# Attention tiles in blocks of 128 neighbouring edges, the feed-forward gathers issued first, and h turned a step later, in a graph network in f32 on one core

## The reference, cut to what matters

```python
# layer 0: attention over edges, softmax over the edges of each dst, then feed-forward
q, k, v = x @ qW + qb, x @ kW + kb, x @ vW + vb
scores = sum(q[src] * k[dst], heads) / 4 + edge_attr @ eW + eb
attn = softmax of scores over the edges with the same dst
out = segment_sum(v[src] * attn, dst) @ oW + ob
x = layer_norm(x + out, ln1_g, ln1_b)
h = gelu(layer_norm(x @ f1W + f1b, lnf_g, lnf_b)) @ f2W + f2b
x = layer_norm(x + h, ln2_g, ln2_b)
# layer 2: h = x @ lin_w.T + lin_b, then three times
agg = segment_sum((h @ weight[i])[src], dst)
h = gru_cell(agg, h)         # r, z = sigmoid(...), n = tanh(in + r * hn), h = (1 - z) * n + z * h
```

## Time and profile before

| what | value |
|---|---|
| median of 3 runs | 6031.04 us (6014.32 to 6034.06) |
| the profiled execution, its own time | 6028.9 us |
| its span, first to last instruction | 6027.0 us |
| attend, about | 210 to 800 us |
| ffn, about | 815 to 1925 us |
| gate0, gate1, gate2, about | 3340 to 3975, 3975 to 4590, 4590 to 5320 us |
| busy in the whole span | PE 71%, DVE 68%, POOL 60%, ACT 49% |
| mean granted clock of PE | 0.867 of full speed |

### The profile page before, as it was taken

One profiled execution on the slowest core, in us unless ns is written; L12 is line 12 of the kernel. 1 busy time (PEld: TensorE's weight loads), 2 busy tenths in 40 slices (PEclk: granted clock), 3 DMA queues, 4 the chain that ended last, 5 costly groups with the idle time before them and its releaser, 6 DMA issues. The chain is left out here.

```text
span 6027.0 us, 75672 instructions
## 1 busy us (share of the span) xinstructions
PE 4279.1 (71%) x16190; PEld 2524.1 (42%) x16190; DVE 4070.7 (68%) x13522; ACT 2924.8 (49%) x6388; POOL 3629.7 (60%) x3234
## 2 busy tenths in 40 slices
PE   6577759999997556546665679967996669836643
PEld 3244434444443333334443445534443334336643
DVE  6576659999997444457775676557665889836633
ACT  0466637777775010146665345534443446536643
POOL 4676558888885888735555660056104757855355
PEclk8788869999998777778887899988998899977877
DMA  6233323333332444456665675457545667757621
GB/s 214 66 85 80 73 70 99 99 99 99 99 99 78 62 62 63 54 141 196 193 190 162 185 211 146 131 160 214 164 141 147 176 159 211 197 162 227 183 78 54
DMA packets 767598, 802.43 MB, mean 133 GB/s; under 512 B 139632, under 2 KB 527800, under 8 KB 767018
## 3 DMA queue, kind: packets, MB, share of 16 engines
q1 hardware_dynamic: 405354, 393.44, 23.5%
q0 software_dynamic: 117504, 209.42, 15.0%
q10 hardware_dynamic: 244288, 194.72, 9.7%
HBM read 445.32 MB, written 351.92 MB: 132 GB/s over the span
## 5 line engine op out<-in xcount | busy, mean ns | idle before, releaser
L462 PE MATMUL gate_bank<-gate_ht,gate_whh 128*128 128x512 f32 x1764 | 874.6, 618 | 32.5 <-DVE gate_n L532 22.2
L925 POOL DMA_INDIRECT xh<-mean_xh,mean_pos_all x392 | 378.0, 964 | 349.0 <-DVE mean_xh L1027 158.9
L462 PEld LDWEIGHTS gate_bank<-gate_ht,gate_whh 128*128 128x128 f32 x1764 | 341.3, 202 | 413.0 <-issue 381.6
L2053 PE MATMUL back_ps_sums<-back_same,back_rows 128*128 128x512 f32 x400 | 289.5, 890 | 285.7 <-DMA back_rows<-x_a,back_idx 285.7
L151 POOL DMA_INDIRECT ffn_rows<-att_sums,ffn_idx x392 | 409.0, 1043 | 114.8 <-issue 106.3
L289 POOL DMA_INDIRECT gate_rows<-h_a,by_pos x200 | 195.8, 979 | 433.3 <-POOLq L117 327.3
L1494 PE MATMUL ffn_ps_f<-ffn_hg,ffn_f 128*128 128x512 f32 x784 | 407.1, 616 | 46.4 <-ACT ffn_hg L1671 46.4
L458 PE MATMUL gate_bank<-by_rank,gate_win 128*128 128x512 f32 x882 | 435.1, 593 | 0.0
L1487 PE MATMUL ffn_ps_u<-ffn_xs_t,ffn_up_w 128*128 128x512 f32 x784 | 387.2, 596 | 1.1 <-issue 1.1
L583 ACT ACTIVATE gate_z<-gate_bank,gate_b_rz 128x512 f32<-128x512 f32 x294 | 201.5, 686 | 351.0 <-PE gate_bank L462 221.0
L2034 POOL DMA_INDIRECT back<-back_out,back_dest x200 | 324.3, 1621 | 68.0 <-issue 60.1
(11 more groups left out here) (270 smaller groups left out, 11984.1 us busy)
## 6 DMA issues: line engine op xcount, KB each, us to landing
mean_x<-x_a SPq DMA_DIRECT2D x196, 256.0 KB
back<-blank ACTq DMA_DIRECT2D x99, 264.0 KB, 4.6
mean_rows<-back SPq DMA_DIRECT2D x98, 264.0 KB
hp<-mean_xh SPq DMA_DIRECT2D x98, 264.0 KB
gate_x<-xh SPq DMA_DIRECT2D x98, 264.0 KB
gate_hot<-hot_rows SPq DMA_DIRECT2D x100, 256.0 KB
ffn_x<-in_x_in SPq DMA_DIRECT2D x98, 256.0 KB
ffn_xr<-in_x_in SPq DMA_DIRECT2D x98, 256.0 KB
```

The source lines that it names most:

```text
L462: last = nc.tensor.matmul(bank_[:, :], whh[:, c * D:(c + 1) * D], ht[:, t.slot4, :], start=not inputs, stop=True)
L925: nc.gpsimd.indirect_dma_start(out=g["xh"][:, :], out_offset=bass.IndirectOffsetOnAxis(ap=pos_all[:, t.n, j:j + 1], axis=0), in_=xh[:, t.n ...
L2053: last = nc.tensor.matmul(ps_sums[t.slot][:, :], rows[:, t.slot4, j, :], same[:, t.slot, j, :], start=j == 0, stop=j == J - 1)
```

## The change

In attend, SP loads the indices from a new input `edge_blocks`, which holds the same edges so that gather j fetches the 128 neighbouring edges 128j to 128j+127. Transposes and out product then use dense columns, and the store of `att_sums` uses `part_tile`, four pieces of 512 bytes for each partition. In ffn, POOL's four gathers stand at the head of its step, and DVE makes `xh` with scalar_tensor_tensor, the inverse as a broadcast tensor operand, in the place of tensor_scalar. In the gates, the transposes of h, `out` and the stores move from lag 2 to lag 3, `hn` has four buffers, and in the final round what comes behind (power, shifts, scatter) moves a step too.

```diff
@@ gated_layer
-        d, hn = (f.sb(s, [P, 2, SUPER]) for s in ("d", "hn"))
+        d, hn = f.sb("d", [P, 2, SUPER]), f.sb("hn", [P, 4, SUPER])
...
-                if final and (t := item_at(5)):
+                if final and (t := item_at(6)):
                     ln.rstd(nc, pool, t, y_done)
                 if e := edges_at(0):
                     sums.gather(pool, e)
-                if final and (t := item_at(6)) and t.has:
+                if final and (t := item_at(7)) and t.has:
...
-                if t := item_at(2):
+                if t := item_at(3):
                     wait(pe, h_done, t.n + 1)
                     wait(pe, out_done, t.n)
                     for j in range(J):
                         last = nc.tensor.transpose(ps_out[:, j * D:(j + 1) * D],
-                                                   hn[:, t.slot, j * P:(j + 1) * P], g["ident"][:, :])
+                                                   hn[:, t.slot4, j * P:(j + 1) * P], g["ident"][:, :])
...
-                    wait(dve, h_turned, t.n - 1)
+                    wait(dve, h_turned, t.n - 3)
...
-                if not final and (t := item_at(2)):
+                if not final and (t := item_at(3)):
                     wait(act, h_turned, t.n + 1)
@@ attention_pass
-                                 nm_tile(g["by_dst"], t)).then_inc(idx_loaded[t.slot4], 16)
+                                 g["edge_blocks"][t.n]).then_inc(idx_loaded[t.slot4], 16)
...
-                        nc.tensor.transpose(edge_columns(ps_send[:, :])[:, j, :], send[:, t.slot4, j, :], g["ident"][:, :])
+                        nc.tensor.transpose(ps_send[:, j * P:(j + 1) * P], send[:, t.slot4, j, :], g["ident"][:, :])
...
-                        last = nc.tensor.matmul(ps_out[:, j * D:(j + 1) * D], edge_columns(att[:, t.slot, :])[:, j, :],
+                        last = nc.tensor.matmul(ps_out[:, j * D:(j + 1) * D], att[:, t.slot, j * P:(j + 1) * P],
                                                 ow[:, :], start=True, stop=True)
...
-                    act.dma_start(nm_tile(g["att_sums"], t), out[:, t.slot, :]).then_inc(stored[t.slot], 16)
+                    act.dma_start(part_tile(g["att_sums"], t.n, 0, D),
+                                  out[:, t.slot, :].rearrange("p (j d) -> p j d", j=J)).then_inc(stored[t.slot], 16)
@@ ffn_pass
             def step(tile_at):
+                if t := tile_at(0):
+                    gather_step(nc, pool, t, idx, rows, g["att_sums"], idx_loaded, a_done, gathered)
                 if t := tile_at(2):
...
-                if t := tile_at(0):
-                    gather_step(nc, pool, t, idx, rows, g["att_sums"], idx_loaded, a_done, gathered)
...
-                        last = nc.vector.tensor_scalar(xh[:, t.slot4, j, :], a[:, t.slot4, j, :],
-                                                       mv[:, root_slot(t, LN1), LN1, j, 0:1], inverse(t, LN1)[:, j:j + 1],
-                                                       ALU.subtract, ALU.mult)
+                        last = nc.vector.scalar_tensor_tensor(
+                            xh[:, t.slot4, j, :], a[:, t.slot4, j, :], mv[:, root_slot(t, LN1), LN1, j, 0:1],
+                            inverse(t, LN1)[:, j:j + 1].broadcast_to([P, D]), ALU.subtract, ALU.mult)
```

More of the change, by code:

```diff
@@ L372, in gated_layer @@
         ht_loaded = f.sems("ht_loaded", 4)
[L373 removed]
+        stored, ht_stored = f.sems("stored"), f.sems("ht_stored", 4)
         r_made, z_made, nh_made, ni_made, h_turned = (
@@ L415, in step @@
                     sums.store_hots(sp, e)
-                if final and (t := item_at(5)) and t.has:
+                if final and (t := item_at(6)) and t.has:
                     wait(sp, stored[t.m % 2], 16 * (t.m // 2 + 1))
@@ L420, in step @@
                                  ).then_inc(back_loaded[t.m % 4], 16)
-            over_items(5 if final else 0, step)
+            over_items(6 if final else 0, step)
             if initial:
@@ L444, in step @@
                             in_=back_x[:, t.m % 4, j, :], in_offset=None).then_inc(back_scattered[t.m % 4], 16)
-            over_items(6, step)
+            over_items(7 if final else 0, step)
             if final:
@@ L498, in step @@
                     sums.sum(pe, e)
-            over_items(2, step)
+            over_items(3, step)
         @block.vector
@@ L533, in step @@
                                                    ALU.add, ALU.mult).then_inc(n1_done, 1)
-                if final and (t := item_at(5)):
+                if final and (t := item_at(6)):
                     ln.shifts(nc, dve, t, y_done)
-                if final and (t := item_at(2)):
+                if final and (t := item_at(3)):
                     wait(dve, h_turned, t.n + 1)
@@ L556, in step @@
                     nc.vector.tensor_copy(g["node_at"][:, HT:NT, :], g["tails"][:, HT:NT, :, 0]).then_inc(ids_made, 1)
-            over_items(5 if final else 2, step)
+            over_items(6 if final else 2, step)
         @block.scalar
@@ L572, in step @@
                                          ).then_inc(id_done, 1)
-                if final and (t := item_at(6)):
+                if final and (t := item_at(7)):
                     wait(act, stored[t.slot], 16 * t.u)
@@ L576, in step @@
                              [y[:, t.slot, j, :] for j in range(J)], y_done)
-                if not final and (t := item_at(2)):
+                if not final and (t := item_at(3)):
                     wait(act, h_done, t.n + 1)
-                    act.dma_start(ht_out[t.tile], hn[:, t.slot, :]).then_inc(ht_stored[t.slot], 16)
+                    act.dma_start(ht_out[t.tile], hn[:, t.slot4, :]).then_inc(ht_stored[t.slot4], 16)
                 if t := item_at(1):
@@ L602, in step @@
                     nc.scalar.activation(ht[:, t.slot4, :], ps_in[:, :], ACT.Copy).then_inc(ht_made, 1)
-                if final and (t := item_at(6)):
+                if final and (t := item_at(7)):
                     wait(act, y_done, t.n + 1)
                     act.dma_start(part_tile(x_out, t.tile, 0, D), y[:, t.slot, :, :]).then_inc(stored[t.slot], 16)
-            over_items(6 if final else 2, step)
+            over_items(7 if final else 3, step)
             for b in range(2):
                 act.wait_ge(stored[b], 16 * (NT // 2))
-                if not final:
-                    act.wait_ge(ht_stored[b], 16 * (NT // 2))
+            if not final:
+                for b in range(4):
+                    act.wait_ge(ht_stored[b], 16 * ((NT - b + 3) // 4))
 class Turn:
@@ L1198, in step @@
                     for j in range(J):
-                        last = nc.tensor.transpose(edge_columns(ps_recv[:, :])[:, j, :], recv[:, t.slot4, j, :],
+                        last = nc.tensor.transpose(ps_recv[:, j * P:(j + 1) * P], recv[:, t.slot4, j, :],
                                                    g["ident"][:, :])
```

6 lines of the change are left out of this document (4 added, 2 removed).

## The result

The changed kernel takes 6059.42 us at the median of 7 runs (6049.81 to 6071.95), the kernel before 6031.04 us (6004.67 to 6038.52, also 7 runs, timed in turn with it). The ratio is 1.0059, with a 95% interval of 1.0045 to 1.0074: it is slower, where I had forecast no change. The profiled execution has a span of 6066.3 us against 6027.0.

The account below looks back on a forecast made before the run. The prediction took ffn as bound by POOL, attend by a PE-ACT ring and gate1's second half by PE. Attend 0, ffn +15 and gates -13 summed to +2 us on the profiled 6028.9, forecast 6031; range 5975 to 6062.

Parts of the forecast that it names:

- What bounds the kernel: Whole kernel: ffn bound by POOL, attend by a ring of PE and ACT, gate1's second half by PE.
- ffn, order: ffn: POOL's step keeps the same instructions, only what lies under what moves; +19 us, bounds -42 to +34.
- The contention term: ffn: POOL's first two gathers take 1.26 us each under two-input DVE operations, 0.19 us a step more, +19 us.
- ffn, xh: ffn: xh takes 2.0 us a step less of DVE, hidden by POOL except at the phase's ends; -4 us.
- Attend: Attend: 50 us less PE work only makes PE more idle ahead of q; 0 us.
- the 0.07 of the upper bound: Attend: PE's mean clock of 0.81 could fall by 0.07 under lighter load, for +15 us.
- case C: Slower: PE's clock falls in attend, +15 us, about 0.74 downwards decisive; with ffn at +34, 6065 us; 22%.
- Gates: All gate rounds: turns, out and stores a step later, terms summing to -13 us.
- gate1's -15: gate1's first half: opening the ring through PE's turn removes a third of the possible 45 us in long steps.
- gate2's -3: gate2's first half: DVE's bound, idle 50 of 355 us, waits for a turn only part of that; -3 us.
- The scatter's +3: gate2's end: POOL's scatters start a step later; +3 us, between 0 and +6.
- The sum: Whole kernel: attend 0, ffn +15, gates -13, together +2 us, forecast as no change.

## Why the prediction was wrong

**What bounds the kernel** held: ffn is POOL's (an edit on DVE alone moved the step by 0.19 us and no more), attend is not PE's (42 us off PE moved nothing), gate1's second half is PE's.

**The step that failed is "ffn, order."** I wrote that POOL's sum of a step is the same instructions, moved them against DVE's work, and priced only what lies under what. I did not move them against SP's queue, so POOL's wait for its indices stood in the sum at nothing, without a reason. Between `xb`, which releases the xr load and with it the indices queued behind, and the gathers that need those indices, the old order left a whole step; the new one leaves a power. The wait is 0.85 us in a plain step and 83.0 in all, and the step went up by 0.62 on average (median 0.32). The run with the xr load moved shows it by taking it off (0.9939), and the run with it brought on in the old order shows it without moving a gather (+280 us). The mean lies above the median because in some steps the indices land later still: the longest wait is 2.50 us in the changed kernel and 1.94 in the row of the order alone. The queue could have been read before the run. In the old trace SP issued xr at 1400.07, right behind the end of `xb` at 1398.74 + 1.25 = 1399.99, and the indices at 1400.49, when the first gather of that step (1400.17) had started; so these indices were the next step's.

**The contention term** had the wrong sign. I took +0.19 a step; the gathers' sum went from 4.22 to 3.94 on average, so -0.28. Two inputs on DVE over a gather's start do not make it 1.26.

**ffn, xh.** Off POOL's path, as written, apart from 14 us of gain by its own (0.9977; 2 to 26 by its interval) through the second gather. But I gave the freed 2.0 us of DVE to both edits together, and it belongs to the order. The rule that I cited from the Trainium skill (GPSIMD Engine Reference, Key points), contention with DVE instructions in a 2-port perf mode or with two SBUF inputs, held where I used it least: `xh`, whose new form has two SBUF inputs, waits for POOL's additions. So does the old form, tensor_scalar; in which mode it runs no row shows. What that sentence does not tell, the runs show: it is DVE that is held here, a first `xh` of up to 2.53 us in the one form and 2.59 in the other, and POOL's additions stay at medians of 1.25 to 1.28.

**Attend**: 0 forecast, 1.0003 measured. The 50 us of PE time were 42, and reappear as idle time ahead of q. The clock went from 0.81 to 0.79 in the phase, not down by the 0.07 of the upper bound, and case C's 0.74 did not come.

**Gates**: -13 forecast, -21 (-30 to -12) measured. The sum is inside the interval partly by luck, since its terms were off both ways. gate1's -15 was about -8: with the turn a step later the ring is open, but the plain step stays 5.1, since DVE's own work fills it (memset 0.48, four additions 1.55, d, d2, hn 0.68, 0.69, 0.71, n1 0.74 and a gap of 0.19 are 5.04 in the changed kernel's timeline); the long steps stayed, 7 above 8 us in each of the two traces. gate2's -3 was -12: its plain step went from 7.4 to 7.3 and the steps of 7.9 are nearly gone, and which of DVE's waits held them was not measured apart. The scatter's +3 was +6. What the trace shows for these, some -14, is less than the ratio's middle value; the rest is not placed.

**The sum**: 0 + 15 - 13 on record; by the runs 0 + 51 - 14 - 21 = +16 for the parts alone, and +36 for the whole. The parts do not add up with the order in: `xh`'s gain comes from a gather that the new order has shortened already (0.97), so without its 14 the sum is +30, which the interval of the whole (27 to 45) holds. Case C, slower, had the right sign with the wrong mechanism.

## What to carry to other kernels

When instructions of one engine are reordered, list for each what releases it, and for each DMA among the releasers what stands ahead of it in its queue and which instruction releases that. A load that waits for a buffer holds all the loads behind it, and the distance between the instruction that frees the buffer and the one that needs the next load is what a reordering changes. Put the small load that the next step needs first ahead of the load that waits for something late.

When two engines are both full, ask which one's operations are stretched: a mean of 801 ns with a shortest of 329 says that it waits inside the instruction, and the edit that ends this is to move the other engine's work away, not to change the form. It pays only where the held engine is on the path. Here POOL was the bound: DVE's `xh` lost its stretch and no time was gained by that, and with the xr load moved too the stretch went to `var`.

## What the runs showed of the hardware

- DVE operations in SBUF, tensor_scalar of 128x128 (up to 2.53 us instead of 0.33), scalar_tensor_tensor with two SBUF operands (2.59), and tensor_scalar of only 128x16 (`var`, a median of 2.09 in the run with the xr load a step later instead of 0.17), are held until POOL's tensor_tensor operations that run beside them end: each long one ends 0.04 to 0.16 us behind such an end (95 of 95 in the kernel before, 98 of 98 with the new form, 87 of 87 `var`). Two that follow each other on POOL hold it through both. POOL's own are not longer for it (medians of 1.25 to 1.28 in all kernels). Not held beside the same additions, in the changed kernel: the aggregation of the norms (291 of 0.14 to 0.18 us) and `u`, which reads one of its two tensors from PSUM (323 of 0.34 to 0.35).
- A load of 2 KB of indices on SP's queue lets POOL's gather start 3.25 us after its issue in a plain step, and up to 4.91 us in others of the changed kernel.
- A gather's issue on POOL in a plain step of ffn takes 0.94 to 1.27 us. The long value comes 0.69 us into `z` when `xh` ahead of it is a tensor_scalar, and not (1.01 to 1.04) when it is a scalar_tensor_tensor.
